# Index tiles transposed by DMA instead of TensorE, and the low parts of h on GpSimd, in an attention block with a look-up FFN

## The chip, the cores and the metric

The kernel runs on one core of a Trainium2 chip. The metric is the device time of one execution in microseconds. The program is written in Bass, with every semaphore and every SBUF address placed by hand.

## The reference

```python
def attention(x, Wq, Wk, Wv, Wo):            # x: 2 x 2048 x 512, weights 512 x 512
    q, k, v = x @ Wq, x @ Wk, x @ Wv
    qT, kT, vT = (swapaxes(a, 1, 2) for a in (q, k, v))
    w = softmax(einsum('bes,bfs->bef', qT, kT) / sqrt(16))     # 512 x 512, over features
    return swapaxes(einsum('bef,bfs->bes', w, vT), 1, 2) @ Wo

def ffn(x, lut, gate_idx, up_idx, down_idx): # indices 0..15, int32
    gate = x @ lut[gate_idx].T               # 512 -> 1376
    up = x @ lut[up_idx].T
    return (silu(gate) * up) @ lut[down_idx].T

x = x + attention(layernorm(x), Wq, Wk, Wv, Wo)
x = x + ffn(layernorm(x), lut, gate_idx, up_idx, down_idx)
```

## The kernel before

The scores are 512 x 512 over features, so they follow from the Gram matrix of the normalised x, and the whole attention of a batch folds into one matrix m of 512 x 512. Every matrix is kept as a high and a low part in a 32-bit matmul format, and every product is three matmuls (high x high and the two mixed ones).

**The gram stage** (about 10 to 98 us) takes the 4096 tokens in 8 blocks `g` of four tiles, 32 tiles `i` in all. For a tile VectorE takes the statistics (`stats_of`, L1185), GpSimd the reciprocal root for a block (`root`, L717, `rstd`), ScalarE normalises (`gram_n`, L854) and rounds to the high part (`gram_in`, L861), VectorE makes the low part (`gram_low`, L1227), and TensorE adds 12 matmuls to the Gram matrix (L1061). Batch 0 is tiles 0 to 15, batch 1 tiles 16 to 31. The Gram matrix is symmetric; its missing blocks come from the `mirror` stage (L1075).

**The product stage** (about 98 to 211 us) is 36 products `n` of 12 matmuls (L960): PROD, SCORE with the softmax, the turned Wv, MIX and FOLD for both batches. SyncE loads the raw weights Wk, Wq, Wo (`load_raw`), Wv and x.

**The paired stage** (about 211 to 378 us) runs the FFN of the first two blocks of 512 tokens together, in an order written out by hand (`first_plan`): `G5` is gate and up of chunk 5 for block 0 (24 matmuls, L1018), `H5` the same for block 1, `D5` the down product for block 0 (12 matmuls, L1026). There are 11 chunks of 128 rows of the 1376. For each G or H ScalarE takes silu (L912), VectorE multiplies by up (`h_full`, L1418), ScalarE rounds (`h_high`, L926), VectorE makes the low part (`h_low`, L1424, recorded in the helper at L1227). SyncE stores the parts of block 1 to DRAM and loads them later. From about 400 us on the six other blocks run in the plain form, where GpSimd makes the low part (L712).

**The weight look-up** makes 33 weight tiles `u` (gate, up, down of 11 chunks) out of 4-bit indices and is spread over the gram, product and paired stages. For a tile ScalarE makes 7 and VectorE one of the eight "leaves" (part or picked = table entry + step x high bit, L753 and L1252), VectorE finds the bits of the index (L1215, L1223) and merges the leaves with 7 predicated copies (L1208), ScalarE rounds the result to `w_hi` (L768) and VectorE makes `w_lo` (L1227): 13 steps on VectorE. `G5` needs the `w_lo` of tiles 16 and 17 (counted from 1) and `G10` of 31 and 32, `D10` of 33.

**How an index tile came to it.** The indices lie in DRAM with the wrong axis in the rows. GpSimd loads a tile with a cast from int32 to bf16 (`load_idx`, L709, 16 buffers `idx_bf`), TensorE turns it with four small transposes against a bf16 identity (L1047, L1049), ScalarE copies it from PSUM to uint8 (L846), the first three tiles straight into `idx_in`, the rest into `idx_out`, which SyncE stores to `idx_scratch` (L557); ScalarE's queue fetches each tile three tiles ahead of its use (`fetch_idx`, L746).

**The order of the work** is one list, `timeline`; each engine walks through it and does its share of each entry. The look-up steps of ScalarE and VectorE are put in between by two strings of digits, `ACT_LOOKS` and `DVE_LOOKS`: digit k is the number of steps ahead of entry k. An engine runs ahead of the list's other engines as far as its semaphores allow.

```python
            for _ in range(idx_per_tile[i]):
                timeline += ([("idx_load", u + IDX_AHEAD)] if u + IDX_AHEAD < U else []) + [("idx", u)]
                u += 1
            timeline.append(("gram", i))
```

Of the kernel before, what the change touches and what calls it, by code (L numbers as in the profile page):

```python
# [6 lines left out]
ACT = mybir.ActivationFunctionType  # L7
# [3 lines left out]
BF16 = mybir.dt.bfloat16  # L11
I16 = mybir.dt.int16
I32 = mybir.dt.int32
U8 = mybir.dt.uint8

P = 128
# [4 lines left out]
def preln_attention_ghost_ffn(nc, x_in, wq_in, wk_in, wv_in, wo_in, lut_in, gate_in, up_in, down_in, out):  # L21
# [25 lines left out]
    U = 3 * C  # L47
    MIRROR_ITEM = 2
# [6 lines left out]
    with ctx:  # L55
# [44 lines left out]
        xg = [at(f"xg{i}", kib, [P, T, D], F32) for i, kib in enumerate((76, 84, 156))]  # L100
# [3 lines left out]

        idx_bf = [at(f"idx_bf{i}", 92 + 1 * i, [P, D], BF16) for i in range(16)]
        idx_out = [at(f"idx_out{i}", 176 + i / 2, [P, D], U8) for i in range(4)]
# [7 lines left out]
        ident_bf = at("ident_bf", 204.5, [P, P], BF16)  # L114
# [18 lines left out]
        idx_dram = nc.dram_tensor("idx_scratch", (U, P, D), U8).ap()  # L133
        m_dram = nc.dram_tensor("m_scratch", (B, 2, P, K * D), F32).ap()
# [11 lines left out]
        idx_loaded = [sem(f"idx_loaded{i}") for i in range(16)]  # L146
        idx_turned = sem("idx_turned")
        idx_laid = sem("idx_laid")
        idx_stored = [sem(f"idx_stored{i}") for i in range(4)]
# [6 lines left out]
        idx_cleared = sem("idx_cleared")  # L156
# [6 lines left out]
        xg_loaded = [sem(f"xg_loaded{i}") for i in range(3)]  # L163
# [140 lines left out]
        idx_per_tile = [(0, 1, 2, 2)[i % 4] if i < T * GB else (i >= T * GB + 4) + (i == T * NG - 1) for i in range(T * NG)]  # L304
        assert sum(idx_per_tile) == U
        MIRROR_AT = T * NG - 4
        U_HIGH_BANKS = sum(idx_per_tile[0:T * GB])
        U_BEFORE_MIRROR = sum(idx_per_tile[0:MIRROR_AT])
        AHEAD = 2
        IDX_AHEAD = 8  # L310
# [5 lines left out]
        timeline += [("idx_load", u) for u in range(IDX_AHEAD)]  # L316
        u = 0
        for i in range(T * NG):
# [27 lines left out]
        for n in range(K, LAST_ITEM):  # L346
# [71 lines left out]
        for step in second_plan:  # L418
# [72 lines left out]

# [983 lines left out]
```

## Time and profile before

| | |
|---|---|
| median of 3 runs | 1046.42 us (1044.93 to 1046.98) |
| the profiled execution | 1046.57 us |
| its span in the trace | 1044.6 us, 12958 instructions |
| TensorE busy | 1010.1 us (97%) |
| VectorE, ScalarE, GpSimd busy | 485.5, 465.3, 134.5 us |
| chain that ended last | PE 80%, DVE 9%, ACT 5%, issue 3%, DMA 1%, POOL 1% |

In the profile PE is TensorE, PEld its weight loads, DVE is VectorE, ACT ScalarE, POOL GpSimd, SP SyncE; a q behind a name is the engine's queue or sequencer. The ends of matmuls are modelled and reach over the start of the next, so a busy PE is not one that is at its peak: what a matmul costs in a row of them is read from start to start. The same holds in a smaller way for ScalarE and VectorE, whose operations overlap the one before by some 0.1 us. The span is divided by stages: gram to 98.5, products to 211.4, paired to some 380, plain blocks to the end. The granted clock of TensorE is 0.994 of full speed.

### The profile page before, as it was taken

To read this page: it belongs to the slowest core of one execution; us is meant where nothing else is said; L and a number is where in the kernel's file an instruction comes from. 1 tells how busy PE (TensorE), PEld (TensorE's weight loads), DVE (VectorE), ACT (ScalarE), POOL (GpSimd) and SP (SyncE) were. 2 spreads that over 40 slices of the span, in tenths; PEclk is the share of its full clock that TensorE was granted. 3 is DMA by queue.
4 is the path that set the end of the run, shared out by engine and by line. 5 is a ranking of instruction groups with operands and counts; after the bars stand their busy time and mean duration, and the time that the engine had idled before them with its cause. 6 is when DMAs were issued, how large, how long until landed. Compare 5 with 4: busy or idle time off the path is not lost.

```text
span 1044.6 us, 12958 instructions
## 1 busy us (share of the span) xinstructions
PE 1010.1 (97%) x4744; PEld 833.8 (80%) x4744; DVE 485.5 (46%) x1019; ACT 465.3 (45%) x753; POOL 134.5 (13%) x136
## 2 busy tenths in 40 slices
PE   5979999999999999999999999999999999999998
PEld 4878877878788868888888887888888888888886
DVE  5897998989999942311131113111311131112001
ACT  5999998797899921221222122212221222122111
POOL 5410000000000000110111011101110111011111
PEclk9999999999999999999999999999999999999999
DMA  9963012031011182200220002002200020001001
GB/s 239 200 170 103 21 54 89 6 129 46 29 71 49 66 317 86 101 1 1 81 81 1 1 1 82 1 1 81 81 1 1 1 81 1 1 1 41 1 1 40
DMA packets 31756, 61.42 MB, mean 59 GB/s; under 512 B 8704, under 2 KB 19152, under 8 KB 27344
## 3 DMA queue, kind: packets, MB, share of 16 engines
q1 hardware_dynamic: 18432, 54.40, 14.2%
q0 software_dynamic: 8944, 4.24, 3.5%
q10 hardware_dynamic: 4320, 1.97, 0.7%
q8 instruction: 39, 0.64, 0.3%
q14 instruction: 21, 0.17, 0.1%
HBM read 43.98 MB, written 20.84 MB: 62 GB/s over the span
## 4 chain that ended last, share of the span: by engine, by line
PE 80%; DVE 9%; ACT 5%; issue 3%; DMA 1%; POOL 1%; ACTq 0%; POOLq 0%; SPq 0%; DVEq 0%
PE bank L1018 44%; PE bank L1026 21%; PE bank L960 10%; DVE part L1208 2%; PE bank L1061 2%; DVE bn L1185 1%; PE bank L974 1%; DVE picked L1208 1%; PE bank L1007 1%; ACT part L753 1%; ACT xg_n L854 1%; ACT idx_out L846 1%; DVE xg_lo L1227 1%; DMA xg<-in_L_attn_x 1%; POOL rstd L717 1%
## 5 line engine op out<-in xcount | busy, mean ns | idle before, releaser
L1018 PE MATMUL bank<-x2t_hi,w_hi 128*128 128x512 f32 (+1 forms) x704 | 275.2, 391 | 3.8 <-DVE x2t_lo L1305 3.5
L1018 PE MATMUL bank<-x2t_hi,w_lo 128*128 128x512 f32 (+1 forms) x704 | 274.8, 390 | 0.0
L1018 PE MATMUL bank<-x2t_lo,w_hi 128*128 128x512 f32 (+1 forms) x704 | 274.7, 390 | 0.0
L1432 DVE TENSOR_TENSOR h_full<-bank,h_gate 128x512 f32<-128x512 f32 (+1 forms) x66 | 45.6, 691 | 396.5 <-PE bank L1018 396.5
L753 ACT ACTIVATE part<-high_bit,lut,lut_step 128x512 f32<-128x512 uint8 x198 | 154.5, 812 | 14.2 <-DVE part L1208 8.6
L1018 PEld LDWEIGHTS bank<-x2t_hi,w_hi 128*128 128x128 f32 (+1 forms) x704 | 130.8, 186 | 34.0 <-issue 4.7
L1018 PEld LDWEIGHTS bank<-x2t_lo,w_hi 128*128 128x128 f32 (+1 forms) x704 | 130.9, 186 | 29.6
L1018 PEld LDWEIGHTS bank<-x2t_hi,w_lo 128*128 128x128 f32 (+1 forms) x704 | 130.8, 186 | 29.2
L933 ACT ACTIVATE h_gate<-bank 128x512 f32<-128x512 f32 (+1 forms) x66 | 39.5, 598 | 256.5 <-PE bank L1018 256.5
L712 POOL TENSOR_TENSOR h_lo<-h_full,h_hi 128x512 fp32r<-128x512 f32 (+1 forms) x66 | 85.3, 1292 | 507.9 <-ACT h_hi L936 507.9
L1026 PE MATMUL bank<-w_hi,h_hi 128*128 128x512 f32 (+1 forms) x324 | 129.6, 400 | 0.1
L1026 PE MATMUL bank<-w_lo,h_hi 128*128 128x512 f32 (+1 forms) x324 | 126.6, 391 | 0.0
L1026 PE MATMUL bank<-w_hi,h_lo 128*128 128x512 f32 (+1 forms) x324 | 126.3, 390 | 0.0
L936 ACT CAST h_hi<-h_full 128x512 fp32r<-128x512 f32 (+1 forms) x66 | 41.0, 621 | 188.3 <-DVE h_full L1432 188.3
L1208 DVE COPY_PREDICATED part<-bit_mask,part 128x512 f32<-128x512 uint8 x132 | 97.9, 742 | 6.8 <-ACT part L753 6.8
L717 POOL TENSOR_TENSOR rstd<-var,power 128x4 f32<-128x4 f32 x20 | 22.4, 1120 | 388.8 <-DVE var L1198 388.8
L1208 DVE COPY_PREDICATED picked<-bit_mask,part 128x512 f32<-128x512 uint8 x99 | 71.0, 740 | 1.0 <-ACT picked L753 0.7
L1026 PEld LDWEIGHTS bank<-w_lo,h_hi 128*128 128x128 f32 (+1 forms) x324 | 60.8, 188 | 13.2
L1026 PEld LDWEIGHTS bank<-w_hi,h_hi 128*128 128x128 f32 (+1 forms) x324 | 60.9, 188 | 12.1 <-POOL h_lo L712 0.5
L1026 PEld LDWEIGHTS bank<-w_hi,h_lo 128*128 128x128 f32 (+1 forms) x324 | 61.0, 188 | 11.7
L1061 PE MATMUL bank<-xg_hi 128*128 128x256 f32 (+2 forms) x128 | 45.2, 353 | 16.7 <-DVE xg_lo L1227 14.6
L960 PE MATMUL bank<-m_hi,xt_hi 128*128 128x512 f32 x112 | 43.7, 390 | 0.0
(151 smaller groups left out, 1329.9 us busy)
## 6 DMA issues: line engine op xcount, KB each, us to landing
xg<-in_L_attn_x SPq DMA_DIRECT2D x7, 1024.0 KB, 6.8
x1a<-in_L_attn_x SPq DMA_DIRECT2D x4, 1024.0 KB, 4.9
out_dram<-x1a SPq DMA_DIRECT2D x4, 1024.0 KB, 3.9
x1b<-in_L_attn_x SPq DMA_DIRECT2D x3, 1024.0 KB, 4.9
m_hi<-m_scratch SPq DMA_DIRECT2D x3, 1024.0 KB, 4.8
m_lo<-m_scratch SPq DMA_DIRECT2D x3, 1024.0 KB, 6.9
out_dram<-x1b SPq DMA_DIRECT2D x3, 1024.0 KB, 3.9
h_scratch<-h_kept_hi SPq DMA_DIRECT2D x10, 256.0 KB, 2.0
```

The lines of the kernel that those rows point to most:

```text
L712: return pool.tensor_tensor(out_, whole, high.bitcast(F32), ALU.subtract)
L717: pool.tensor_tensor(scale[:, tiles], var[:, tiles], power[:, tiles], ALU.pow).then_inc(rstd_made, 1)
L753: act.activation(tile, high, ACT.Identity, bias=entry, scale=step).then_inc(leaf_made, 1)
L846: act.copy(dst, src).then_inc(idx_laid, 1)
L933: act.activation(h_gate[0:n, :], bank[4][0:n, :], ACT.Silu).then_inc(silu_done, 1)
L936: act.copy(h_hi[c % 2][0:n, :], h_full[0:n, :]).then_inc(h_hi_done, 1)
L960: last = pe.matmul(out_, a, b, start=(i == 0 and j == 0), stop=(i == len(terms) - 1 and j == 2))
L1018: last = pe.matmul(tile[0:n, :], a, x, start=(k == 0 and j == 0), stop=(k == K - 1 and j == 2))
L1026: last = pe.matmul(bank[t][:], a, x, start=start and j == 0, stop=stop and j == 2)
L1061: last = pe.matmul(bank[4 * batch + m][:, cols], a[:, rows_of], b[:, cols], start=start and j == 0, stop=stop and j == 2)
L1208: return dve.copy_predicated(keep[:], bit_mask[bit][:], other[:])
L1432: dve.tensor_tensor(h_full[0:n, :], bank[5][0:n, :], h_gate[0:n, :], ALU.mult).then_inc(h_done, 1)
```

## The change

The index tiles are no longer turned by TensorE. GpSimd first copies the indices from DRAM to DRAM with a cast to uint16, in six parts (`narrow`, 19 transfers in all: gate, up and down of chunks 0, 1, 2-3, 4-5, 6-7, 8-10, and a filling of the last chunk of down). SyncE then issues for each tile a transposing transfer of 2-byte elements from DRAM to one of eight buffers `idx_wide` (`turn_idx`), and GpSimd stores it with a cast to uint8 to `idx_scratch`, or for the first three straight into `idx_in` (`store_idx`). The transposes on TensorE, the 33 copies on ScalarE, the 33 loads by `load_idx`, the 30 stores of SyncE, the bf16 identity and four memsets go. The space that comes free holds a fourth buffer for x in the gram stage. In the paired stage the low part of h is made by GpSimd, as it was in the later blocks. Both strings of look-up steps are new.

```diff
+    NARROW = [slice(0, 1), slice(1, 2), slice(2, 4), slice(4, 6), slice(6, 8), slice(8, C)]
-        xg = [at(f"xg{i}", kib, [P, T, D], F32) for i, kib in enumerate((76, 84, 156))]
+        xg = [at(f"xg{i}", kib, [P, T, D], F32) for i, kib in enumerate((76, 84, 156, 92))]
...
+        narrow_at = [2, 10, 16, 24, 30, 34]
+        turn_at = [9, 10, 11, 16, 18, 20, 22, 24, 26, 28, 29, 30] + list(range(31, 52))
+        store_at = [place + 2 for place in turn_at]
...
-            for _ in range(idx_per_tile[i]):
-                timeline += ([("idx_load", u + IDX_AHEAD)] if u + IDX_AHEAD < U else []) + [("idx", u)]
-                u += 1
+            index_steps(i)
             timeline.append(("gram", i))
...
+            index_steps(T * NG + n - K)
             timeline.append(("take", n))
...
+            def turn_idx(u):
+
+                c, kind, slot = u // 3, u % 3, u % len(idx_wide)
+                if kind == 0:
+                    for part_, run in enumerate(NARROW):
+                        if run.start == c:
+                            sp.wait_ge(idx_narrowed[part_], 16 * (4 if run.stop == C else 3))
+                if u >= len(idx_wide):
+                    sp.wait_ge(idx_stored[slot], times_stored(u - len(idx_wide)))
+                n = rows(c)
+                if kind < 2:
+                    src = (gate_dram, up_dram)[kind][c * P:c * P + n, :]
+                    dst = idx_wide[slot][:].rearrange("p (k o) -> p k o", k=K)[:, :, 0:n]
+                else:
+                    src, dst = down_dram[:, c * P:(c + 1) * P], idx_wide[slot][:]
+                sp.dma_start(dst, src, transpose=True).then_inc(idx_turned[slot], 16)
...
+            def narrow(part_):
+
+                run, done = NARROW[part_], idx_narrowed[part_]
+                span = slice(run.start * P, min(run.stop * P, I))
+                for src, dst in ((gate_in, gate_dram), (up_in, up_dram)):
+                    pool.dma_start(dst[span, :], src[span, :]).then_inc(done, 16)
+                pool.dma_start(down_dram[:, span], down_in[:, span]).then_inc(done, 16)
...
+            def store_idx(u):
+
+                slot = u % len(idx_wide)
+                pool.wait_ge(idx_turned[slot], times_stored(u))
+                dst = idx_in[u][:] if u < STRAIGHT else idx_dram[u]
+                pool.dma_start(dst, idx_wide[slot][:]).then_inc(idx_stored[slot], 16)
...
+                if stage == "h_low":
+                    b, c = arg
+                    n, q = rows(c), pair_count[arg]
+                    hi, lo = h_kept if b else (h_hi[c % 2], h_lo[c % 2])
+                    pool.wait_ge(h_hi_done, q)
+                    low(lo[0:n, :], h_full[0:n, :], hi[0:n, :]).then_inc(h_lo_done, 1)
...
-                    act.copy(dst, src).then_inc(idx_laid, 1)
...
-                    for k in range(K):
-                        if kind < 2:
-                            last = pe.transpose(turned[:, k * P:k * P + n], idx_bf[u % len(idx_bf)][0:n, k * P:(k + 1) * P], ident_bf[0:n, 0:n])
-                        else:
-                            last = pe.transpose(turned[0:n, k * P:(k + 1) * P], idx_bf[u % len(idx_bf)][:, k * P:k * P + n], ident_bf[:])
-                    last.then_inc(idx_turned, 1)
```

A place up to 31 is ahead of the gram tile of that number, from 32 on ahead of product n = place - 28. How this moves instructions, first on GpSimd's queue in the gram stage (`gate_scratch` and the like are the DRAM copies; `rstd` are the reciprocal roots of a block, for which VectorE and then ScalarE wait). Before:

```order
L717 TENSOR_TENSOR rstd_kept_190<-var,power 128x3 [waits var_made]
L709 DMA idx_bf_142<-in_L_ffn_gate_idx 128x512
L709 DMA idx_bf_143<-in_L_ffn_up_idx 128x512
L709 DMA idx_bf_144<-in_L_ffn_down_idx 128x4x128
L709 DMA idx_bf_145<-in_L_ffn_gate_idx 128x512
```

Now, from the first narrowing on:

```order
L708 DMA gate_scratch<-in_L_ffn_gate_idx 16x4096
L708 DMA up_scratch<-in_L_ffn_up_idx 16x4096
L709 DMA down_scratch<-in_L_ffn_down_idx 512x128
L726 TENSOR_TENSOR rstd_174<-var,power 128x4 [waits var_made]
L726 TENSOR_TENSOR rstd_175<-var,power 128x4 [waits var_made]
L708 DMA gate_scratch<-in_L_ffn_gate_idx 16x4096
L708 DMA up_scratch<-in_L_ffn_up_idx 16x4096
L709 DMA down_scratch<-in_L_ffn_down_idx 512x128
L718 DMA idx_in_163<-idx_wide_143 128x512 [waits idx_turned0]
L726 TENSOR_TENSOR rstd_174<-var,power 128x4 [waits var_made]
```

The loads went ahead of the roots without a wait on another engine's work; the stores wait for the transposing transfers and have roots behind them.

On SyncE's queue, behind the gram stage, the tail that ends with the load of x1a (the x of block 0 for the layer norm, which ScalarE reads in MIX). Before:

```order
L557 DMA idx_scratch<-idx_out_161 128x512 [waits idx_laid]
L557 DMA idx_scratch<-idx_out_158 128x512 [waits idx_laid]
L563 DMA raw_124<-in_L_attn_Wo 128x512 [waits raw_lo_done]
L563 DMA raw_123<-in_L_attn_Wo 128x512 [waits raw_lo_done]
L563 DMA raw_124<-in_L_attn_Wo 128x512 [waits raw_lo_done]
L594 DMA x1a<-in_L_attn_x 128x2048
```

Now:

```order
L576 DMA raw_124<-in_L_attn_Wo 128x512 [waits raw_lo_done]
L570 DMA_TRANSPOSE idx_wide_145<-down_scratch 128x512 [waits idx_stored2]
L576 DMA raw_123<-in_L_attn_Wo 128x512 [waits raw_lo_done]
L570 DMA_TRANSPOSE idx_wide_146<-gate_scratch 128x4x128 [waits idx_stored3]
L576 DMA raw_124<-in_L_attn_Wo 128x512 [waits raw_lo_done]
L570 DMA_TRANSPOSE idx_wide_147<-up_scratch 128x4x128 [waits idx_stored4]
L570 DMA_TRANSPOSE idx_wide_148<-down_scratch 128x512 [waits idx_stored5]
L570 DMA_TRANSPOSE idx_wide_149<-gate_scratch 128x4x96 [waits idx_stored6]
L570 DMA_TRANSPOSE idx_wide_150<-up_scratch 128x4x96 [waits idx_stored7]
L570 DMA_TRANSPOSE idx_wide_143<-down_scratch 128x512 [waits idx_stored0]
L605 DMA x1a<-in_L_attn_x 128x2048
```

Transposing transfers stand where stores stood, and eight of them follow the second of these loads of Wo.

On VectorE in the paired stage one stretch between two low parts of weights. Before:

```order
L1208 COPY_PREDICATED part_167<-bit_mask_171,part_168 128x512 [waits own_leaf_made,leaf_made]
L1227 TENSOR_TENSOR h_kept_lo<-h_full,h_kept_hi 128x512 [waits h_hi_done]
L1227 TENSOR_TENSOR w_lo_67<-picked_163,w_hi_56 128x512 [waits w_hi_done]
L1208 COPY_PREDICATED part_164<-bit_mask_171,part_166 128x512 [waits leaf_made]
L1208 COPY_PREDICATED picked_162<-bit_mask_172,part_165 128x512 [waits merged,bits_found]
```

Now:

```order
L1187 COPY_PREDICATED part_156<-bit_mask_160,part_157 128x512 [waits own_leaf_made,leaf_made]
L1206 TENSOR_TENSOR w_lo_67<-picked_152,w_hi_56 128x512 [waits w_hi_done]
L1187 COPY_PREDICATED part_153<-bit_mask_160,part_155 128x512 [waits leaf_made]
L1187 COPY_PREDICATED picked_151<-bit_mask_161,part_154 128x512 [waits merged,bits_found]
L1187 COPY_PREDICATED part_156<-bit_mask_161,part_153 128x512 [waits merged]
```

The low parts of h are gone from between the look-up steps; all else of the look-up is as it was, at other places.

## Rows read from the trace of the kernel before

**Rows 1.** Windows: stretch, length; PE, PEld, DVE, ACT, POOL busy (x); PEclk, DMA share, GB/s.
```profile
18.60:54.40 35.80, 32.39 (x236) 29.49 (x236) 28.56 (x69) 35.73 (x63) 15.36 (x22) 1.00 1.08 214
54.40:98.50 44.10, 38.74 (x255) 34.87 (x256) 37.33 (x89) 42.90 (x76) 7.14 (x8) 0.96 0.52 141
98.50:211.40 112.90, 107.27 (x490) 87.79 (x489) 106.44 (x219) 99.36 (x170) 1.40 (x1) 0.98 0.13 47
211.40:281.10 69.70, 67.71 (x305) 55.55 (x306) 62.91 (x130) 59.54 (x91) 1.01 (x1) 0.98 0.15 59
281.10:365.80 84.70, 84.70 (x376) 69.82 (x375) 84.47 (x176) 77.48 (x117) 0.00 (x0) 1.00 0.18 64
```

**Rows 2.** Chain of waits up to 280 us: start, us, what.
```profile
21.25 3.92 PE bank L1061 x24
...
86.89 0.63 PE bank L1079 x4
89.66 1.99 PE bank L1061 x12
...
98.48 2.76 PE bank L960 x12
```

**Rows 3.** Timelines of VectorE, TensorE at 365 us: start, us, engine, line, operation.
```profile
364.91 0.68 DVE L1227 TENSOR_TENSOR w_lo<-picked,w_hi 128x512 fp32r<-128x512 f32 x1
...
366.23 0.39 PE L1018 MATMUL bank<-x2t_hi,w_hi 128*96 128x512 f32 x1
```

**Rows 4.** Timeline of ScalarE in the gram stage.
```profile
31.26 0.84 ACT L854 ACTIVATE xg_n<-xg,shift,rstd 128x512 f32<-128x512 f32 x1
31.98 0.63 ACT L861 CAST xg_hi<-xg_n 128x512 fp32r<-128x512 f32 x1
32.48 0.61 ACT L846 CAST idx_out<-bank 128x512 uint8<-128x512 bf16 x1
32.96 0.85 ACT L753 ACTIVATE part<-high_bit,lut,lut_step 128x512 f32<-128x512 uint8 x1
```

**Rows 5.** Groups of instructions, 0 to 520 us: busy us, mean ns | idle before.
```profile
L846 ACT CAST idx_out<-bank 128x512 uint8<-128x512 bf16 (+2 forms) x30 | 17.0, 580 | 0.5 <-PE bank L1049 0.4
```

**Rows 6.** Timeline of VectorE in the paired stage.
```profile
282.75 0.67 DVE L1227 TENSOR_TENSOR w_lo<-picked,w_hi 128x512 fp32r<-128x512 f32 x1
283.34 0.74 DVE L1208 COPY_PREDICATED part<-bit_mask,part 128x512 f32<-128x512 uint8 x1
283.98 0.66 DVE L1227 TENSOR_TENSOR h_kept_lo<-h_full,h_kept_hi 128x512 fp32r<-128x512 f32 x1
284.58 0.73 DVE L1208 COPY_PREDICATED picked<-bit_mask,part 128x512 f32<-128x512 uint8 x1
...
290.55 0.67 DVE L1227 TENSOR_TENSOR w_lo<-picked,w_hi 128x512 fp32r<-128x512 f32 x1
```

**Rows 7.** Page, costliest groups: the low part of h on GpSimd, later blocks.
```profile
L712 POOL TENSOR_TENSOR h_lo<-h_full,h_hi 128x512 fp32r<-128x512 f32 (+1 forms) x66 | 85.3, 1292 | 507.9 <-ACT h_hi L936 507.9
```

**Rows 8.** Timelines of VectorE, then GpSimd, about three of its small operations.
```profile
44.79 0.76 DVE L1208 COPY_PREDICATED picked<-bit_mask,part 128x512 f32<-128x512 uint8 x1
45.44 0.72 DVE L1208 COPY_PREDICATED part<-bit_mask,part 128x512 f32<-128x512 uint8 x1
...
44.34 1.44 POOL L717 TENSOR_TENSOR rstd<-var,power 128x4 f32<-128x4 f32 x1 [5.37 <-DVE var L1198]
...
55.37 1.03 POOL L717 TENSOR_TENSOR rstd<-var,power 128x4 f32<-128x4 f32 x1 [6.42 <-DVE var L1198]
...
79.20 1.58 POOL L717 TENSOR_TENSOR rstd<-var,power 128x4 f32<-128x4 f32 x1 [5.97 <-DVE var L1198]
```

**Rows 9.** DMA issues: out<-in, queue, count, KB each, median us to landing.
```profile
idx_scratch<-idx_out SPq DMA_DIRECT2D x30, 64.0 KB, 3.7
...
idx_bf<-in_L_ffn_down_idx POOLq DMA_DIRECT2D x10, 128.0 KB, 4.9
```

**Rows 10.** Timeline of ScalarE, first use of x1a.
```profile
156.27 0.85 ACT L809 ACTIVATE xn_first<-x1a,shift_kept,rstd_kept 128x512 f32<-128x512 f32 x1
```

More of the change, by code:

```diff
@@ L10 @@
 F32R = mybir.dt.float32r
-BF16 = mybir.dt.bfloat16
 I16 = mybir.dt.int16
+U16 = mybir.dt.uint16
 I32 = mybir.dt.int32
@@ L103, in preln_attention_ghost_ffn @@
         xg_n = [at(f"xg_n{i}", 164 + 2 * i, [P, D], F32) for i in range(4)]
-        idx_bf = [at(f"idx_bf{i}", 92 + 1 * i, [P, D], BF16) for i in range(16)]
-        idx_out = [at(f"idx_out{i}", 176 + i / 2, [P, D], U8) for i in range(4)]
+        idx_wide = [at(f"idx_wide{i}", 172 + i, [P, D], U16) for i in range(8)]
         picked = [at("picked0", 188, [P, D], F32), at("picked1", 190, [P, D], F32)]
@@ L145, in preln_attention_ghost_ffn @@
         rstd_made = sem("rstd_made")
[L146 to L149, printed above, removed]
+        idx_narrowed = [sem(f"idx_narrowed{i}") for i in range(len(NARROW))]
+        idx_turned = [sem(f"idx_turned{i}") for i in range(len(idx_wide))]
+        idx_stored = [sem(f"idx_stored{i}") for i in range(len(idx_wide))]
         idx_back = [sem(f"idx_back{i}") for i in range(3)]
@@ L162, in preln_attention_ghost_ffn @@
         xg_first_loaded = [sem(f"xg_first_loaded{t}") for t in range(T)]
-        xg_loaded = [sem(f"xg_loaded{i}") for i in range(3)]
+        xg_loaded = [sem(f"xg_loaded{i}") for i in range(len(xg))]
         xg_stats = sem("xg_stats")
@@ L302, in normalised, with index_steps @@
             timeline.extend([("norm", n), ("norm_low", n)])
[L304 to L305 removed]
+        narrow_at = [2, 10, 16, 24, 30, 34]
+        turn_at = [9, 10, 11, 16, 18, 20, 22, 24, 26, 28, 29, 30] + list(range(31, 52))
+        store_at = [place + 2 for place in turn_at]
+        assert len(narrow_at) == len(NARROW) and len(turn_at) == U
+        def index_steps(place):
+            timeline.extend(("narrow", part_) for part_, at_ in enumerate(narrow_at) if at_ == place)
+            timeline.extend(("idx_turn", u) for u, at_ in enumerate(turn_at) if at_ == place)
+            timeline.extend(("idx", u) for u, at_ in enumerate(store_at) if at_ == place)
         MIRROR_AT = T * NG - 4
[L307 to L308 removed]
         AHEAD = 2
[L310 removed]
         timeline.append(("stats_of", (0, 0)))
@@ L684, in _ @@
             pool.memset(ident[:], 0.0).then_inc(const_made, 1)
-            pool.memset(ident_bf[:], 0.0).then_inc(const_made, 1)
-            for tile in idx_out:
-                pool.memset(tile[:], 0).then_inc(idx_cleared, 1)
-            pool.wait_ge(const_made, 2)
-            for one in (ident, ident_bf):
-                pool.affine_select(out=one[:], in_=one[:], compare_op=ALU.not_equal, fill=1.0, base=0,
-                                   pattern=[[-1, P]], channel_multiplier=1).then_inc(const_made, 1)
+            pool.wait_ge(const_made, 1)
@@ L1418, in _ @@
                     dve.tensor_tensor(h_full[0:n, :], pair_bank(arg)[1][0:n, :], h_gate[0:n, :], ALU.mult).then_inc(h_done, 1)
-                if stage == "h_low":
-                    b, c = arg
-                    n, q = rows(c), pair_count[arg]
-                    hi, lo = h_kept if b else (h_hi[c % 2], h_lo[c % 2])
-                    dve.wait_ge(h_hi_done, q)
-                    low(lo[0:n, :], h_full[0:n, :], hi[0:n, :]).then_inc(h_lo_done, 1)
             def ffn(b):
```

132 lines of the change are left out of this document (43 added, 89 removed).

## The prediction

> **What bounds the kernel now.** I read the windows first, then the chain of waits, then the timelines of ScalarE, VectorE and GpSimd. From 18.6 to 98.5 us (the gram stage) ScalarE is busy 35.73 of 35.80 and 42.90 of 44.10 us, VectorE 28.56 and 37.33 [rows 1]. TensorE looks busy too, but its gram work is less than the stage: one tile is 12 matmuls, two tiles take 3.92 us, 1.96 each, and the 29 tiles from the fourth on took 77.2 us (from 21.25 to the first product at 98.48) where 29 x 1.96 are 56.8 [rows 2]. So this stage goes at ScalarE's pace. Behind it TensorE is idle for 5.6 us up to 211.4, 2.0 up to 281.1 and not at all up to 365.8, while VectorE is busy 106.44 of 112.90, 62.91 of 69.70 and 84.47 of 84.70 us [rows 1]: from 281 on both are full. The weight look-up and TensorE meet at one point: the low part of weight tile 32 is made at 364.91 to 365.59 and the matmuls that need it (up of chunk 10, `G10`) begin at 366.23, 0.6 us later [rows 3]. A later VectorE, or an earlier TensorE, makes TensorE wait there. After that point the look-up is over and nothing that the change touches limits TensorE.
>
> **The gram stage.** ScalarE loses 33 copies of turned index tiles, 0.48 us each from start to start (32.48 to 32.96), 15.8 us in all [rows 4, 5]. TensorE loses the 132 small transposes. It would then be TensorE's own pace that binds: 56.8 us for 29 tiles, 2.8 for the mirror (86.89 to 89.66) [rows 2], and some 2 us for tiles 16 to 23, where ScalarE still has more than TensorE: a tile's two steps cost 0.72 + 0.50 us and a leaf 0.72 [rows 4]; eight tiles (9.8), four takes (1.4), four splits of raw weights (2.0) and six leaves (4.3) make 17.5 us against 8 x 1.96 = 15.7. Sum 61.6 where it was 77.2, so the stage ends at 82.9: **-15.6 us** for all that follows on TensorE. No gain, and 17.6 if those 2 us vanish, are the ends of this term.
>
> **What the gram stage gives up.** In VectorE's order 48 look-up steps stood ahead of the first product and now 22 do: 26 steps, two index tiles. One index tile costs VectorE 6.0 us: from one low part of a weight to the next are 7.80 us, and in it lie two h_low and one h_full of 0.60 each [rows 6]. So 12.0 us of VectorE work move behind the gram stage.
>
> **h_low.** 19 of the 22 low parts of h come before the low part of weight tile 32. On VectorE each takes 0.60 us from start to start (283.98 to 284.58) [rows 6]: -11.4 us, which all but pays for the deferred tiles. On GpSimd one takes 1292 ns [rows 7], 0.7 us later for who waits; TensorE's down of a chunk comes at least one item of 5.4 us or more behind it, and the store of h_kept has the rest of an item: nothing. Counted from the front, VectorE's work up to weight tile 32 falls by 11.4 us and its idle time in the gram stage from 14.0 us to 10.4 (from 18.6, 64.3 us of stage less 65.9 - 12.0 of work) [rows 1]. Weight tile 32 could be ready at 365.6 - 11.4 - 3.6 = 350.6, and TensorE would want it at 366.2 - 15.6 = 350.6. Without anything else the two fit again.
>
> **Does GpSimd hold VectorE up?** The trace has no long GpSimd operation beside look-up steps, so this is bounded. The small rstd on GpSimd takes 1.03 us with no two-input VectorE operation beside it (55.37) but 1.44 and 1.58 at 44.34 and 79.20, where a merge or a low part had just begun: longer by about the rest of that operation. The other way the merges at 44.79 and 45.44 started 0.65 us apart, against 0.63 otherwise: VectorE was hardly held, but rstd reads four elements [rows 8]. An h_low reads 2 x 512. The ends for the hold per h_low are 0 (as those merges) and 1.29 us (the whole operation [rows 7]). I take **0.9**: seven merges of 0.63 and a low part of 0.60 are 5.0 of a tile's 6.0 us, so five times in six a two-input operation is next, and the reading is less than the whole operation. I am nearer the upper end because GpSimd did wait for all of VectorE's operation. 19 x 0.9 = +17.1 us, of which the six items up to 281 (5.4 us) can fall into VectorE's 6.8 us of idle time there [rows 1]. Weight tile 32 then comes at 350.6 + 17.1 - 5.4 = 362.3, and TensorE starts `G10` up there rather than at 366.2: **-3.9 us**.
> The Trainium skill (SBUF — State Buffer, section Who interferes with whom) goes further: a VectorE instruction with two SBUF inputs and a GpSimd instruction that reads SBUF share one read interface, and the second to come is blocked for all of the first. The trace agrees in one direction (1.44 and 1.58 against 1.03) and doesn't show the other; by the whole rule the hold would be 1.29.
>
> **The new way of the indices.** GpSimd issues 19 narrowing transfers and 33 stores where it issued 33 loads; SyncE issues 33 transposing transfers where it issued 30 stores. First tile: rstd of block 1 done at about 18, three issues, landing 4.9, a transposing transfer at 3.7 to 6.8, a store behind the rstd of block 3 and the second narrowing at about 34, landing 3.7 [rows 9]: in place at 38 to 41. VectorE's first look stands ahead of low part 15, at about 41: nothing, up to 3 us if the loads crowd it. Each store waits on GpSimd's queue with the rstd of a later block behind it; from tile 3 on the stores have one to three gram tiles (2 to 6 us) after their transfer is issued. The trace shows no transposing transfer. Twenty-one of them stand behind the gram stage in SyncE's queue, mixed with three loads of Wo and ahead of that of x1a, which ScalarE used at 156.27 [rows 10] and would use at 140. From 80 to 135 there are 2.6 us for each. The lower end is nothing, the upper 3.7 us if each waited for a landing as long as the old stores' [rows 9]; I take under 2.6, since 8 buffers let them overlap.
> By the Trainium skill (DMA: Bandwidth & Descriptors, section Latency and other measured facts) a transposing transfer moves 261 GB/s; 128 KB would be an estimated 0.5 us, 21 of them 10 us, and nothing would be late.
>
> **Sum**, against the profiled execution of 1046.57 us (span 1044.6 and 2.0 around it; 0.15 above the median): 1046.57 - 3.9 = **1042.7**.
>
> **Rivals.**
> (A) The forecast: the gram stage gains 16 us and VectorE, held by GpSimd, gives most of it back at the end of the look-up. Own range 1038 to 1048 (hold 0.7 to 1.1, first index tile up to 3 us late). Chance 0.50.
> (B) VectorE isn't held: TensorE's 350.6 binds and all 15.6 us stay, less some 1.5 for handovers between two full engines: 1032.5. For it: the merges at 44.79 and 45.44. Against: the stretched rstd. 0.25.
> (C) The full hold, 1.29 us for each of 19 h_low, of which 4 are absorbed: 350.6 + 24.5 - 4 = 371.1, 4.9 later than now: **1051.5**. It decides from (366.2 - 350.6 + 5.4) / 19 = 1.11 us per h_low. For it: GpSimd's waits in the other direction; against: the reading is only a part of the operation. 0.13. By the page on SBUF of the Trainium skill this is the case to expect.
> (D) Transposing transfers are slow. It decides from 2.6 us each; at 3.7 the x1a arrives at 80 + 78 + 5 = 163, 23 us after ScalarE wants it: 1046.6 - 16 + 23 = 1054, more at a slower rate. 0.09.
> (E) No effect: the look-up's start is so late that VectorE's end stays at 365.6. 0.03.
>
> **How the numbers follow.** No change here means within 0.2% (2.1 us), about what a measurement of this kernel can tell. Faster: of A the part below 1044.3, 0.32, B 0.25 and 0.01 of D: 0.58. Same: 0.11 of A, 0.03 of E: 0.14. Slower: 0.07 of A, 0.13 of C, 0.08 of D: 0.28. The range reaches from 1030 (B) to 1053 (C and the mildest of D); outside lie about 0.03 below and 0.1 above.
>
> **What would show it.** Right: no idx_out copies, gram tiles 2.0 us apart, the first product at 82 to 84 us; merges and low parts of w beside an h_low stretched, or started late, by 0.7 to 1.1 us; h_low on GpSimd at 1.3 to 2 us; a wait of TensorE in `G8` to `G10` for the low part of w of some 12 us in all; x1a loaded before 140. Wrong: merges at 0.63 us throughout and no wait at `G10` (B); VectorE waiting for the first index tile; ScalarE's xn_first waiting for a DMA (D); or a gram stage that still ends after 90 us, which would mean that ScalarE's copies weren't what set its pace.

## The result and the profile after

The changed kernel takes 1042.91 us (median of 20 runs, 1041.15 to 1045.12), the kernel before 1044.94 us (20 runs, 1042.99 to 1046.98). The ratio is 0.9979, with an interval of 0.9971 to 0.9986: 2.2 us faster, 1.5 to 3.0. The profiled execution of the change took 1041.55 us, with a span of 1039.7 us where that of before was 1044.6. The kernel before has quicker and slower executions (1042.8 to 1043.4 us at a mean granted clock of 0.999, 1046.3 to 1047.0 at 0.994), and its profiled one, 1046.57 us at 0.994, is one of the slowest.

The windows of the changed kernel, over the stretches of [rows 1] (length, then busy us of PE, PEld, DVE, ACT and POOL):

```profile
18.60:54.40 35.80, 35.65 (x221) 32.99 (x221) 30.92 (x78) 29.69 (x51) 10.52 (x15) 1.00 0.81 187
54.40:98.50 44.10, 42.89 (x240) 37.88 (x239) 40.78 (x92) 39.28 (x67) 16.17 (x26) 1.00 1.07 168
98.50:211.40 112.90, 105.92 (x484) 86.44 (x483) 105.49 (x216) 102.47 (x172) 12.51 (x18) 0.98 0.39 98
211.40:281.10 69.70, 66.69 (x306) 54.88 (x305) 65.34 (x132) 59.04 (x88) 19.94 (x8) 1.00 0.11 38
281.10:365.80 84.70, 76.72 (x316) 61.48 (x315) 83.27 (x152) 70.59 (x107) 28.24 (x11) 0.94 0.15 53
```

In the first stretch ScalarE fell from 35.73 to 29.69 us and TensorE rose to 35.65 of 35.80. In the last TensorE, busy without a gap before, has 8.0 us of idle time. The granted clock there is 0.94 where it was 1.00: behind a wait of 3.91 us that ends at 339.07, TensorE's matmuls start 0.43 us apart up to 344.78 (the lower of its two clock levels) and 0.23 apart after that. This cost nothing at `G10`, for which TensorE waited again.

The chain of waits, start of the gram stage and its end (start, us, what):

```profile
18.31 27.26 PE bank L1044 x168
...
66.72 4.15 PE bank L1044 x24
...
71.96 7.72 PE bank L1044 x48
79.68 5.47 PE bank L962 x24
```

168 matmuls in 27.26 us are 14 tiles of 1.95 us with nothing between them. The first product starts at 79.68, where it was 98.48 [rows 2]: 18.8 us earlier.

The waits of TensorE in the last stretch (waited for, us in total, times, longest), and the timelines of VectorE and TensorE at the point of [rows 3]:

```profile
PE bank L1020 <- DVE w_lo L1206: 7.9, 2, 3.9
```

```profile
360.64 0.68 DVE L1206 TENSOR_TENSOR w_lo<-picked,w_hi 128x512 fp32r<-128x512 f32 x1
...
361.37 0.48 PE L1020 MATMUL bank<-x2t_hi,w_hi 128*96 128x512 f32 x1
```

So of 18.8 us 4.9 are left where the look-up ends (366.23 to 361.37). Behind that point the two profiles take the same: 1044.6 - 366.23 = 678.4 and 1039.7 - 361.37 = 678.3 us.

The groups of instructions (busy us, mean ns | idle before), first GpSimd's over the whole program:

```profile
L721 POOL TENSOR_TENSOR h_lo<-h_full,h_hi 128x512 fp32r<-128x512 f32 (+1 forms) x77 | 108.3, 1406 | 579.1 <-ACT h_hi L938 507.5 <-ACT h_hi L928 71.6
L721 POOL TENSOR_TENSOR h_kept_lo<-h_full,h_kept_hi 128x512 fp32r<-128x512 f32 (+1 forms) x11 | 29.4, 2668 | 54.8 <-ACT h_kept_hi L928 54.8
```

then VectorE's from 203 to 366 us:

```profile
L1187 DVE COPY_PREDICATED part<-bit_mask,part 128x512 f32<-128x512 uint8 x78 | 59.5, 763 | 2.2 <-ACT part L770 2.2
L1187 DVE COPY_PREDICATED picked<-bit_mask,part 128x512 f32<-128x512 uint8 x59 | 52.0, 905 | 0.0
L1206 DVE TENSOR_TENSOR w_lo<-picked,w_hi 128x512 fp32r<-128x512 f32 x21 | 15.1, 719 | 0.6 <-ACT w_hi L785 0.5
L1231 DVE TENSOR_SCALAR part<-high_bit,lut_step,lut 128x512 f32<-128x512 uint8 x19 | 13.1, 687 | 0.0
```

In the kernel before the same four groups on VectorE have means of 742, 741, 683 and 540 ns in that stretch. The excess is 78 x 0.021 + 59 x 0.164 + 21 x 0.036 + 19 x 0.147 = 14.9 us. It lies in few operations: of the 19 h_low, 13 hold one VectorE operation each by 0.9 to 1.1 us (ten merges and three leaves), one holds a merge by 0.4 us, one makes h_full wait 1.2 us, and four hold next to nothing (0.1 us at most). Beside two of those four VectorE ran operations with one input in SBUF and the other in PSUM, at their usual length (x_second at 222.90 in 0.70 us, two x2t_lo from 246.00 in 1.28). One place with a hold, first VectorE, then GpSimd:

```profile
265.06 0.73 DVE L1187 COPY_PREDICATED part<-bit_mask,part 128x512 f32<-128x512 uint8 x1
265.69 0.68 DVE L1206 TENSOR_TENSOR w_lo<-picked,w_hi 128x512 fp32r<-128x512 f32 x1
266.28 0.73 DVE L1187 COPY_PREDICATED part<-bit_mask,part 128x512 f32<-128x512 uint8 x1
266.91 0.72 DVE L1187 COPY_PREDICATED picked<-bit_mask,part 128x512 f32<-128x512 uint8 x1
267.54 0.72 DVE L1187 COPY_PREDICATED part<-bit_mask,part 128x512 f32<-128x512 uint8 x1
268.16 0.21 DVE L1194 TENSOR_SCALAR bit_mask<-idx_in 128x256 int16<-128x256 int16 x1
268.29 1.84 DVE L1187 COPY_PREDICATED picked<-bit_mask,part 128x512 f32<-128x512 uint8 x1
270.03 0.68 DVE L1397 TENSOR_TENSOR h_full<-bank,h_gate 128x512 f32<-128x512 f32 x1
```

```profile
265.61 3.91 POOL L721 TENSOR_TENSOR h_kept_lo<-h_full,h_kept_hi 128x512 fp32r<-128x512 f32 x1 [3.74 <-ACT h_kept_hi L928]
273.16 3.25 POOL L721 TENSOR_TENSOR h_kept_lo<-h_full,h_kept_hi 128x512 fp32r<-128x512 f32 x1 [3.64 <-ACT h_kept_hi L928]
277.96 1.81 POOL L721 TENSOR_TENSOR h_lo<-h_full,h_hi 128x512 fp32r<-128x512 f32 x1 [1.56 <-ACT h_hi L928]
```

GpSimd's operation starts at 265.61 beside a row of merges at their usual 0.72 us and ends at 269.52, 1.36 us after VectorE's first instruction with one input (268.16). The merge right behind that one is the stretched one, 1.84 us. So the two exclude each other both ways: GpSimd stays out while VectorE runs one two-input operation after another, and holds the next one up when it gets in. At what point it gets in isn't settled. Counted back 1.29 us from its end, six of the 19 h_low get in at such an operation with one input and three just ahead of a leaf, but three between two merges, as here (VectorE, then GpSimd):

```profile
345.81 0.74 DVE L1187 COPY_PREDICATED part<-bit_mask,part 128x512 f32<-128x512 uint8 x1
346.43 1.84 DVE L1187 COPY_PREDICATED picked<-bit_mask,part 128x512 f32<-128x512 uint8 x1
```

```profile
346.02 1.64 POOL L721 TENSOR_TENSOR h_lo<-h_full,h_hi 128x512 fp32r<-128x512 f32 x1 [8.90 <-ACT h_hi L928]
```

### The profile page after: what moved, and what is told of

Read it like the earlier page. It is cut to its first block, busy times and chain, and to the rows that moved or that the text cites. A ratio compares the mean times of both kernels' runs of the same rounds, so it can differ in the third digit from the quotient of the medians.

```text
span 1039.7 us, 12623 instructions
## 1 busy us (share of the span) xinstructions
PE 1001.7 (96%) x4612; PEld 825.9 (79%) x4612; DVE 486.7 (47%) x997; ACT 450.1 (43%) x720; POOL 192.7 (19%) x171
## 4 chain that ended last, share of the span: by engine, by line
PE 75%; DVE 12%; issue 5%; ACT 4%; POOL 2%; DMA 1%; POOLq 0%; ACTq 0%; SPq 0%; DVEq 0%
PE bank L1020 38%; PE bank L1028 20%; PE bank L962 11%; PE bank L1044 4%; DVE part L1187 3%; DVE picked L1187 1%; DVE bn L1164 1%; ACT part L770 1%; PE bank L976 1%; DVE part L1231 1%; PE bank L1009 1%; POOL h_kept_lo L721 1%; DVE w_lo L1206 1%; POOL rstd L726 1%; DVE bit_mask L1194 1%
## 5 line engine op out<-in xcount | busy, mean ns | idle before, releaser
L721 POOL TENSOR_TENSOR h_lo<-h_full,h_hi 128x512 fp32r<-128x512 f32 (+1 forms) x77 | 108.3, 1406 | 579.1 <-ACT h_hi L938 507.5
L1187 DVE COPY_PREDICATED picked<-bit_mask,part 128x512 f32<-128x512 uint8 x99 | 80.7, 838 | 0.1
L1044 PE MATMUL bank<-xg_hi 128*128 128x256 f32 (+2 forms) x128 | 42.6, 333 | 13.9 <-DVE xg_lo L1206 13.8
```

Source lines behind the costliest of these rows:

```text
L721: return pool.tensor_tensor(out_, whole, high.bitcast(F32), ALU.subtract)
L1044: last = pe.matmul(bank[4 * batch + m][:, cols], a[:, rows_of], b[:, cols], start=start and j == 0, stop=stop and j == 2)
L1187: return dve.copy_predicated(keep[:], bit_mask[bit][:], other[:])
```

## The experiments

Each kernel was timed beside the kernel before on the same chip; 1045.0 to 1045.2 us is that kernel's median in the four batches. "Tile 32" is the start of the low part of weight tile 32 in the profile, where [rows 3] had 364.91.

**h_low back on VectorE (e1).** The branch below moves from GpSimd's program to VectorE's (with VectorE's wait), and one look-up step moves ahead of an h_low.

```diff
-                if stage == "h_low":
...
-                    pool.wait_ge(h_hi_done, q)
-                    low(lo[0:n, :], h_full[0:n, :], hi[0:n, :]).then_inc(h_lo_done, 1)
...
+                if stage == "h_low":
...
+                    dve.wait_ge(h_hi_done, q)
+                    low(lo[0:n, :], h_full[0:n, :], hi[0:n, :]).then_inc(h_lo_done, 1)
```

> The changed kernel with h_low back on VectorE in the paired stage (one look-up step is moved ahead of one h_low, nothing else). Theory H (each h_low on GpSimd holds VectorE up for about 1.05 us, more than the 0.6 us that it saves): VectorE gains 19 x 0.45 = 8.5 us up to weight tile 32, which comes at some 352 us instead of 361; time 1042.9 - 8.5 = 1034 to 1036, so it beats both kernels. Rival L (the look-up steps put off behind the gram stage are what takes the gain back, the hold is small): 11.4 us of work return to a full VectorE, tile 32 at 370 or later, time 1049 to 1053.

Measured: 1059.63 us (ratio 1.0138, 1.0117 to 1.016), tile 32 at 375.77. Neither theory had this. Its waits from 98 to 420 us:

```profile
ACT part L764 <- DVE part L1181: 21.7, 23, 1.9
...
DVE h_lo L1200 <- ACT h_hi L922: 10.3, 11, 2.1
DVE h_kept_lo L1200 <- ACT h_kept_hi L922: 9.7, 11, 1.5
```

VectorE stands 20.0 us in front of h_low, since the changed kernel's order has no look-up step between h_full and h_low, and ScalarE then waits for merges. The order of the look-up is part of the change; this run moved one half of it without the other and can't tell what the hold costs.

**The old way of the indices, h_low on GpSimd (e2).** The kernel before with that one branch moved the other way.

> The kernel before with h_low on GpSimd instead of VectorE in the paired stage, the indices turned as before. H: VectorE loses 19 x 0.45 = 8.5 us and has 5 to 6 us of idle time there, tile 32 late by 3 to 8 us, time 1048 to 1053. L (no hold): VectorE has 11.4 us less to do, TensorE's own pace binds, time within 1 us of the kernel before (1044.9).

Measured: 1053.78 us (1.0081, 1.0067 to 1.0095), tile 32 at 370.88, 6.0 us later, inside the 3 to 8 of H; the time is 0.8 us above its range. VectorE has 19 operations less and is later, so GpSimd's h_low costs it more than the 0.6 us each that it saves: (11.4 + 6.0) / 19 = 0.92 us each. The rival is out. The kept low parts took 2471 ns each on GpSimd here (2668 in the changed kernel).

**One input (e3), and none (e4).** In the changed kernel GpSimd's subtraction is replaced by a copy, then by a fill with zeros; the low part of h is not computed in the paired stage in either.

```diff
-                    low(lo[0:n, :], h_full[0:n, :], hi[0:n, :]).then_inc(h_lo_done, 1)
+                    pool.tensor_copy(lo[0:n, :], h_full[0:n, :]).then_inc(h_lo_done, 1)
```

and in e4

```diff
+                    pool.memset(lo[0:n, :].bitcast(F32), 0.0).then_inc(h_lo_done, 1)
```

> The changed kernel, but GpSimd copies h_full into h_lo (one SBUF input) where it subtracted h_hi (two inputs): the low part of h is not computed in the paired stage. H2 (only operations of both engines with two SBUF inputs hold each other): no stretched merges, tile 32 at 348 to 350 as TensorE allows, time 1031 to 1033. H1 (any GpSimd operation that reads SBUF holds VectorE for its length): merges beside it still 1.5 to 1.8 us, time 1038 to 1043. L: no change, 1042 to 1043.5.

> The changed kernel, but GpSimd fills h_lo with zeros (no SBUF input) in the paired stage: the low part of h is left out there. H1 and H2: no hold, merges at 0.63 to 0.73 us throughout, time 1031 to 1033. If writing alone holds VectorE: merges beside it stretched, time over 1036. L: no change, 1042 to 1043.5.

Measured: 1034.62 us (0.9907, 0.9891 to 0.9922) with one input, 1033.04 us (0.9889, 0.9874 to 0.9904) with none; tile 32 at 352.38 and 351.38. The groups on VectorE from 203 to 366 us, with one input:

```profile
L1187 DVE COPY_PREDICATED part<-bit_mask,part 128x512 f32<-128x512 uint8 x78 | 59.2, 759 | 3.1 <-ACT part L770 3.0
L1187 DVE COPY_PREDICATED picked<-bit_mask,part 128x512 f32<-128x512 uint8 x59 | 45.7, 799 | 0.0
```

and with none:

```profile
L1187 DVE COPY_PREDICATED part<-bit_mask,part 128x512 f32<-128x512 uint8 x78 | 58.1, 745 | 3.5 <-ACT part L770 3.3
L1187 DVE COPY_PREDICATED picked<-bit_mask,part 128x512 f32<-128x512 uint8 x59 | 42.2, 743 | 0.0
L1397 DVE TENSOR_TENSOR h_full<-bank,h_gate 128x512 f32<-128x512 f32 (+1 forms) x21 | 14.5, 690 | 12.3 <-PE bank L1020 11.5 <-issue 0.7
```

An operation of GpSimd that only writes holds nothing (745 and 743 ns, as before). One that reads one input does hold. The mean is nearer to normal than with two inputs (799 ns against 905), but the copy is also shorter, 0.61 us alone against 1.29. A merge beside it, then GpSimd's copies, one alone and one kept out:

```profile
323.84 1.15 DVE L1187 COPY_PREDICATED part<-bit_mask,part 128x512 f32<-128x512 uint8 x1
```

```profile
202.86 0.61 POOL L741 CAST h_lo<-h_full 128x512 fp32r<-128x512 f32 x1 [15.69 <-ACT h_hi L928]
309.70 3.84 POOL L741 CAST h_kept_lo<-h_full 128x512 fp32r<-128x512 f32 x1 [4.56 <-ACT h_kept_hi L928]
```

The held merge starts 1.05 us ahead of the next operation where 0.63 is usual, 0.42 us more: the copy's length less 0.2, as the 1.1 us are the subtraction's 1.29 less 0.2. So H2 ("only two-input operations" of GpSimd) is wrong, and H1's mechanism holds (any GpSimd operation that reads SBUF, for about its length), though not its 1.5 to 1.8 us for a merge; the time lies between the two. Without the hold the program is 9.9 us faster, VectorE waits 11.5 us for TensorE, and TensorE's own pace is nearly reached: its last wait for a low part, at `G10`, is 0.84 us. This is rival B's world, and its number (1032.5) is within 0.6 us of the 1033.04.

**Each h_low twice on GpSimd (e5).**

```diff
+        h_lo_once = sem("h_lo_once")
...
+                    low(lo[0:n, :], h_full[0:n, :], hi[0:n, :]).then_inc(h_lo_once, 1)
+                    pool.wait_ge(h_lo_once, q)
                     low(lo[0:n, :], h_full[0:n, :], hi[0:n, :]).then_inc(h_lo_done, 1)
```

> The changed kernel with GpSimd doing each h_low of the paired stage twice, one behind the other. H (each two-input operation of GpSimd holds VectorE for about 0.5 to 1.1 us): the second costs as much as the first, 9 to 20 us more in all: 1052 to 1063. If the second one falls into the shadow of the first (GpSimd waits for VectorE and not the other way): 1043 to 1046.

Measured: 1062.27 us (1.0157, 1.0142 to 1.0171), tile 32 at 380.07 against 360.64: 19.4 us for 19 more, **1.02 us** each, as H had it. Of the 19.4 us, 16.5 are more busy time of VectorE up to tile 32 (346.38 us against 329.93) and 3.0 more idle time. This is the price of a second h_low right behind the first. That the first costs about as much is supported by e2 (0.92 us each), against 0.60 us when VectorE does it itself.

**Transposing transfers in halves (e7).** Every transposing transfer is issued as two of half the size.

```diff
+                    pieces = [(dst[:, k:k + 2, :], src[:, k * P:(k + 2) * P]) for k in (0, 2)]
...
+                    pieces = [(dst[:, k * P:(k + 2) * P], src[k * P:(k + 2) * P, :]) for k in (0, 2)]
...
-                sp.dma_start(dst, src, transpose=True).then_inc(idx_turned[slot], 16)
+                for dst, src in pieces:
+                    sp.dma_start(dst, src, transpose=True).then_inc(idx_turned[slot], 16)
```

> The changed kernel with every transposing transfer split in two halves (same bytes, twice as many transfers on SyncE). T (SyncE pays 1.2 to 1.3 us for each transposing transfer whatever its size): 22 more behind the gram stage, x1a loaded some 27 us later, at about 153 where ScalarE wants it at 140: 1050 to 1055. Rival (the issue costs by size): x1a as now, no change, 1042 to 1044.

Measured: 1051.02 us (1.0052, 1.0038 to 1.0067). SyncE's issue of x1a moved from 120.86 to 138.73, 17.9 us where T had some 27. The price of a transfer is as T had it, 1.25 us at both sizes: a half occupies the queue as long as a whole. The groups of one source, whole and in halves (shortest, median and longest in ns, then the first and last start in us):

```profile
L570 SPq DMA_TRANSPOSE idx_wide<-gate_scratch x11: 1202/1217/1302, 22.6 to 116.9; - x11
L573 SPq DMA_TRANSPOSE idx_wide<-gate_scratch x22: 1190/1246/2591, 22.8 to 132.3; - x22
```

What T left out is that the queue wasn't full: 20 tiles (not 22) are turned behind the gram stage, and between 80.00 and 120.86 the queue had some 10 us of idle time, 7.3 of them in one gap (95.02 to 102.28), which the added halves fill. And what came late first was another load:

```profile
ACT wa_hi L873 <- DMA raw<-in_L_attn_Wo: 8.4, 1, 8.4
DVE wa_lo L1209 <- ACT wa_hi L873: 7.9, 1, 7.9
```

A tile now costs the queue 2.5 us, near the 2.6 from which rival D decides, and the program is 8.1 us slower. But the late load is the raw Wo, which is mixed in with the transfers, not x1a behind them, whose issue is still ahead of 140. With whole transfers neither load was waited for.

**h_low on VectorE in a better order (e6, e8 to e12).** First by hand (e6): between h_full and h_low as many look-up steps as before (the first row that differs in the table of VectorE's look-up steps; the rows behind it change in the same way):

```diff
-004004006000042010000620000004500000330001000070011000a00000003000300100900000a000300000a22000800000
+004004006000042010000620000004500000330001000070011000a02000001020100100900000a030000000a22000801000
```

> The changed kernel with h_low back on VectorE, and its look-up order mended for that: between h_full and h_low as many look-up steps as the kernel before had there (1 to 5), taken from the steps behind the h_low, so that VectorE doesn't stand still while ScalarE rounds h. H (the first try lost because VectorE stood in front of h_low, and the hold is worth 1.05 us for each h_low): no wait for h_hi over some 5 us in all, tile 32 at 352 to 356, time 1034 to 1038. Rival L (VectorE's 11.4 us of h_low are the loss): tile 32 still at 370 or later, 1050 or more.

Measured: 1045.12 us (0.9993, 0.9982 to 1.0004), tile 32 at 363.62. The waits in front of h_low fell from 20.0 to 3.1 us and the time by 14.5 us. ScalarE still waited 13.6 us for merges (21.7 in e1, 10.3 in the changed kernel), and the result lies between the two theories.

Then all look-up steps were placed anew, by one rule in three kernels (e8: h_low on VectorE, e10: on GpSimd, e9: the kernel before): a step is done when the engine's main work isn't ready, and some are then shifted by trial on durations of the traces. The edits are the two tables of step counts alone, for instance the second row that differs in ScalarE's:

```diff
-0000000000100000000000002000000000000000000006000000000000000003000050100020000300004000020000300004
+0000001011000000000210000000100000200001101000000010000000000120200000110110040000200010200202010210
```

> The changed kernel with h_low on VectorE, and the places of all look-up steps on ScalarE and VectorE chosen anew by one rule: an engine does a look-up step when the main work isn't ready, with some shifting by trial on durations of the traces. H: with h_low on VectorE there is no hold, and the order is no longer made for h_low elsewhere; tile 32 at about 350 to 354, time 1028 to 1035, better than both kernels. Rival L (VectorE's 11.4 us of h_low cost what the hold cost, the order isn't what matters): 1043 to 1047, as e6.

> The changed kernel, h_low on GpSimd, its look-up steps placed by the same rule as in e8, which knows nothing of a hold. H: 19 holds of 1.02 us less the 0.6 us of each h_low leave it 5 to 9 us above e8, 1036 to 1042. Rival N (the hold matters only with the order of the changed kernel, which puts its merges where GpSimd works): within 2 us of e8.

> The kernel before (indices turned on TensorE and copied by ScalarE), its look-up steps placed by the same rule as in e8. If the new way of the indices is worth what the gram stage shows (18.8 us at the first product, less what the look-up can't follow): 1040 to 1044, some 9 to 13 us above e8. If the new places are what gains and the transposing transfers are worth little: within 3 us of e8.

Measured: h_low on VectorE 1035.88 us (0.9914, 0.99 to 0.9928); h_low on GpSimd 1038.78 us (0.9943, 0.9929 to 0.9957); the kernel before 1051.11 us (1.0065, 1.0048 to 1.0082). The first has tile 32 at 349.30, a little earlier than expected, and is 0.9 us above the expected range. Its windows show that TensorE binds:

```profile
211.40:281.10 69.70, 68.21 (x314) 56.08 (x313) 67.95 (x143) 60.41 (x93) 1.39 (x1) 1.00 0.09 31
281.10:365.80 84.70, 84.70 (x375) 68.83 (x374) 75.38 (x154) 66.89 (x103) 0.00 (x0) 1.00 0.22 78
```

In the second stretch VectorE has 9.3 us of idle time and TensorE none. With h_low on GpSimd the time is only 2.9 us more, between the two expectations (5 to 9, and under 2). That most of the hold falls into VectorE's idle time is my reading: the rule gave the two kernels different orders, so it isn't shown. The kernel before did neither of the two things expected of it. It lost 6 us, its first gate and up starting at 217.45 where they did at 211.45, so the rule isn't good for every kernel, and what a better order of that kernel would give stays open. At one and the same rule the new way of the indices with h_low on VectorE is 15.2 us faster than the old one.

In e8 the first product started at 85.21. So the last pair (e11, e12) keeps the changed kernel's placing up to the first product and places the rest anew.

> As e8 (h_low on VectorE, look-up steps placed anew), but up to the first product the look-up steps stay where the changed kernel has them: e8 put more of them ahead and reached its first product at 85.2 us where the changed kernel has it at 79.5. If TensorE's start counts (TensorE was busy without a gap from 281 to 366 in e8): 1031 to 1034. If VectorE's end of the look-up counts: it has the same work behind a shorter stage, 1036 to 1039.

> As e11 but with h_low on GpSimd: the price of GpSimd's h_low in an order that was made for neither. H (19 holds of 1.02 us less 0.6 each, 8 us of VectorE): 5 to 8 us above e11 if VectorE is what binds there; if TensorE binds in e11, as in e8, less: 1 to 4 us above it, as e10 stood 2.9 above e8.

Measured: h_low on VectorE 1034.63 us (0.9901, 0.9882 to 0.9919), the fastest kernel of this study that computes the whole, and 8.3 us faster than the changed kernel by the medians; on GpSimd 1041.84 us (0.9969, 0.9953 to 0.9984), 7.2 above it, as expected. The first lies between its two expectations: its tile 32 (355.55 to 356.25) and TensorE (`G10`'s up at 356.50) meet. The stretch from 281.1 to 365.8 us, with h_low on VectorE and then on GpSimd:

```profile
281.10:365.80 84.70, 84.70 (x375) 68.94 (x374) 80.05 (x162) 71.27 (x108) 0.00 (x0) 1.00 0.20 70
```

```profile
281.10:365.80 84.70, 78.88 (x337) 62.60 (x337) 81.71 (x149) 69.37 (x105) 24.94 (x12) 0.98 0.16 57
```

Tile 32 comes at 355.55 and 361.42. The two orders differ, so the 7.2 us are not the hold alone, but they are near what 19 x (1.02 - 0.60) = 8.0 us lead one to expect. The new order alone gained 1.1 us (1042.91 to 1041.84), and the order of e10 gained 4.1. The profiles differ only ahead of `G10`'s up: it starts at 355.59 in e8, 356.50 in e11 and 362.14 in e12, and behind it they take 678.2, 678.1 and 679.7 us, the kernel before 678.4.

## Why the prediction was right

The forecast was case A, 1042.7 us, and the median is 1042.91, by A's mechanism. Point by point:

- **The gram stage, -15.6 us.** Measured -18.8. The direction holds, and so does it that ScalarE set the pace and TensorE does now. How much of it the copies are was not tried alone: ScalarE lost 33 copies ahead of the first product, but also 14 of 27 leaves that were put off. In e8, which has 23 leaves there and no copies, the first product starts at 85.21, so some 5.5 of the 18.8 us go with ten of the leaves put off and VectorE's steps for the same tiles. The 2 us allowed for tiles 16 to 23, where ScalarE has more than TensorE, didn't show. A tile took 1.93 us in TensorE's timeline (7.72 us for four) and not 1.96. The third and fourth tiles also began 0.3 and 0.7 us earlier with no transposes between them.
- **Twelve us of look-up deferred, 11.4 us of h_low gone from VectorE.** As in the order. That the look-up's end, not TensorE's start, decides holds too: TensorE waited for low parts of w (7.9 us on matmuls, twice).
- **The hold, 0.9 us per h_low.** Measured 0.78 in stretched operations, and 1.02 for a second h_low behind each. This was the term with the widest bounds, 0 to 1.29. The trace agrees only in part with the rule of the Trainium skill (SBUF — State Buffer, Who interferes with whom) that was weighed there: a two-input operation is held, but by some 1.1 us and not by all of 1.29; and VectorE's own leaf, with one full input from SBUF beside two columns, is held as well (three of 19, 1.48 to 1.51 us against 0.54). Its condition, that GpSimd's operation reads SBUF, fits e3 and e4: the copy holds, the fill doesn't.
- **What the prediction left out:** that GpSimd would starve. I forecast 1.3 to 2 us for an h_low there and wrote "nothing" for the latency; the kept ones took 2.7 us on average and 3.95 at most, one of the others 4.16. They made h_full wait 1.2 us once, and nothing else ahead of tile 32 shows in the sum.
- **Tile 32 at 362.3, `G10` -3.9 us.** Measured 361.32 (its end), `G10` -4.9. VectorE's time up to tile 32 can be added up from the windows, before and then after (the third busy time is VectorE's):

```profile
0.00:364.91 364.91, 336.67 (x1691) 282.73 (x1692) 327.67 (x706) 321.62 (x520) 37.12 (x58) 0.99 0.33 91
18.60:98.48 79.88, 71.12 (x491) 64.34 (x492) 65.87 (x157) 78.61 (x138) 22.50 (x30) 0.98 0.77 174
```

```profile
0.00:360.64 360.64, 328.88 (x1563) 275.61 (x1564) 329.93 (x688) 306.63 (x487) 89.15 (x91) 0.98 0.43 104
18.60:79.68 61.08, 59.72 (x371) 55.18 (x371) 53.66 (x131) 51.97 (x88) 19.27 (x28) 1.00 0.89 180
```

| change up to tile 32, us | forecast | measured |
|---|---|---|
| h_low no longer on VectorE | -11.4 | -11.4 (19 x 0.60, taken as forecast) |
| hold | +17.1 | +13.7 (busy time +2.3, less the -11.4) |
| idle time in the gram stage | -3.6 | -6.6 (14.0 to 7.4) |
| all other idle time | -5.4 | +0.1 |
| sum | -3.3 | -4.3 |

The sum is right to 1 us, its terms less so. The hold was 0.72 us per h_low by this count, 3.4 us less in all; the idle time of the gram stage shrank by 3.0 us more; and the step that failed is the absorption: none of the 5.4 us of hold that were to fall into idle time behind the gram stage did. That these errors cancel is luck. Why that idle time stayed wasn't tried.
- **TensorE's waits for low parts of w, "some 12 us in all".** 7.9 us on matmuls, 9.3 on weight loads, which overlap them. Mis-sized.
- **The indices.** In place early enough: the store of the first tile was issued at 33.19 and VectorE looked first at 40.42 without a wait. I took a transposing transfer at under 2.6 us; it costs SyncE's queue 1.2 to 1.3 (28 of 33; the other five 2.3 to 4.6). Twenty of them, not 21, stood behind the gram stage. x1a was issued at 120.86, before 140, and used at 140.12.
- **The level.** The sum stood on one profiled execution of 1046.57 us. The median over 20 runs of that kernel came out at 1044.94. So the forecast gain of 3.7 to 3.9 us is more than the measured 2.2 (1.5 to 3.0), and that the level fits within 0.2 us is luck. The profiled pair differs by 5.0 us, more than the medians do; what differs between executions of one kernel wasn't tried.

Of the rivals, B's price was right and its condition wrong (the fill with zeros gives it); C decides from 1.11 us per h_low with 5.4 us absorbed; the measured hold is 0.72 to 1.02. D was not in play at one transfer per tile. Two halves per tile (2.5 us) bring a loss of its kind, by Wo and not by x1a.

## What to carry to other kernels

Before an elementwise operation is handed from VectorE to GpSimd, price it at what it costs the operations that VectorE goes on with: here an operation of 0.60 us on VectorE cost it 0.9 to 1.0 us when GpSimd did it (0.92 in e2, 1.02 in e5), so it belongs on GpSimd only where VectorE has idle time. When such an operation is moved in a kernel with an order laid out by hand, move the order with it: the same edit gave 1059.6, 1045.1, 1035.9 and 1034.6 us in four orders. And a stage that ends 19 us earlier gives only what the next engine can follow; ask first what that engine has left to do at that point.

## What the runs showed of the hardware

- GpSimd's 1.29 us subtraction of 128x512 takes up to 4.16 us beside a run of VectorE's two-input operations, and holds one VectorE operation up by some 1.1 us when it gets in (1.84 us for a merge of 0.73).
- VectorE's operations with one input in PSUM and one in SBUF weren't held (x2t_lo at 246.00, two in 1.28 us beside an h_low); three of its leaves, with one full SBUF input, were (1.48 to 1.51 us against 0.54).
- A copy of 0.61 us with one input on GpSimd holds a merge by 0.42 us and is itself kept out up to 3.84 us; a fill of 0.53 us holds nothing (picked merges 743 ns, 741 in the kernel before) and isn't kept out (0.61 at most).
- A transposing transfer of 128x512 two-byte elements occupies SyncE's queue for 1.2 to 1.3 us, half of one as long (median 1.24 to 1.25), where most plain ones have 0.32 to 0.58. It lands 4.1 to 5.2 us (medians) after its issue. Five took longer, one of them 3.44 us; why isn't shown:

```profile
22.58 1.30 SPq L570 DMA_TRANSPOSE idx_wide<-gate_scratch  x1
23.93 1.26 SPq L570 DMA_TRANSPOSE idx_wide<-up_scratch  x1
...
80.00 3.44 SPq L570 DMA_TRANSPOSE idx_wide<-up_scratch  x1
```
